# A fused two-layer transformer kernel: another order of work where the second attention meets the dense layers, and a last product in two halves

## The reference, cut to what matters

```python
x = x + _L0_xattn_ref(_layernorm(x), ctx_768, ...)
x = x + _L0_ffn_ref(_layernorm(x), ...)
x = x + _L1_xattn_ref(_layernorm(x), ctx_768, ...)   # 16 heads of 8 channels
x = x + _L1_ffn_ref(_layernorm(x), k0, k1, k2, s0, s1, s2)

def _L1_ffn_ref(x, k0, k1, k2, s0, s1, s2):
    # weights are +1 where k is true and -1 where it is false
    h = jnp.concatenate([x, -x], axis=-1)
    h = s0 * _conn_dense(k0, h)      # 256 -> 512
    h = jax.nn.relu(h) * 2
    h = s1 * _conn_dense(k1, h)      # 512 -> 512
    h = jax.nn.relu(h) * 2
    h = s2 * _conn_dense(k2, h)      # 512 -> 128
    return h
```

## Time and profile before

| what | value |
|---|---|
| median of three runs | 241.98 us |
| the profiled execution, its own time | 242.18 us |
| span of its instructions | 240.4 us |
| TensorE busy | 223.1 us (93%) |
| VectorE busy | 169.7 us (71%) |
| ScalarE busy | 123.0 us (51%) |
| mean granted TensorE clock | 0.998 |

### The profile page before, as it was taken

The page is one execution under the profiler, slowest core; times in us unless marked ns, Lnnn a source line. Parts: engine busy times, 40 slices in busy tenths (PEclk is TensorE's granted clock), DMA queues, the critical chain, the costliest instruction groups (busy, mean ns, idle before and its releaser), DMA issues.

```text
span 240.4 us, 4941 instructions
## 1 busy us (share of the span) xinstructions
PE 223.1 (93%) x1785; PEld 180.7 (75%) x1785; DVE 169.7 (71%) x438; ACT 123.0 (51%) x292; POOL 59.9 (25%) x87
## 2 busy tenths in 40 slices
PE   8988888989799999999999999999799999699993
PEld 8346677888787888898898899777578887477782
DVE  1699985768747796556555558988778887398752
ACT  2644669697864462212312324255356557547651
POOL 3272195006220124433033900260000000220200
PEclk9999999999999999999999999999999999999999
DMA  6940010000000002202102162000000000000002
GB/s 190 246 110 30 3 44 4 0 3 0 0 3 0 3 1 65 55 12 65 52 16 65 43 175 68 1 0 3 0 4 3 0 3 3 0 3 1 0 0 87
DMA packets 11820, 8.18 MB, mean 34 GB/s; under 512 B 2964, under 2 KB 11096, under 8 KB 11800
## 3 DMA queue, kind: packets, MB, share of 16 engines
q1 hardware_dynamic: 11800, 7.91, 12.6%
HBM read 5.81 MB, written 0.52 MB: 26 GB/s over the span
## 4 chain that ended last, share of the span: by engine, by line
PE 71%; DVE 13%; ACT 9%; issue 3%; DMA 2%; SPq 0%; DVEq 0%
PE ps L626 10%; PE ps L798 9%; PE ps L449 8%; PE ps L451 8%; PE ps L450 8%; ACT probs L907 6%; PE ps L540 3%; PE ps L717 3%; PE ps L745 3%; PE ps L445 3%; PE ps L704 3%; PE ps L520 3%; DMA x_sb<-in_x 2%; PE ps L730 2%; PE ps L758 2%
## 5 line engine op out<-in xcount | busy, mean ns | idle before, releaser
L956 ACT ACTIVATE kT<-ps 128x512 f32<-128x512 f32 x32 | 19.1, 598 | 47.4 <-PE ps L451 47.4
L626 PEld LDWEIGHTS ps<-w,kT 128*128 128x128 f32 x256 | 30.9, 192 | 1.2
L626 PE MATMUL ps<-w,kT 128*128 128x128 f32 x256 | 31.0, 275 | 0.0
L1273 DVE TENSOR_TENSOR kT<-ps,kT 128x512 f32<-128x512 f32 x32 | 21.8, 689 | 11.1 <-PE ps L451 8.8
L1280 DVE SCALAR_TENSOR_TENSOR x_sb<-ps,comb,x_sb 128x128 f32<-128x128 f32 x64 | 18.0, 343 | 13.5 <-PE ps L626 13.5
L449 PE MATMUL ps<-xT_hi,w_hi 128*128 128x512 f32 x64 | 26.7, 417 | 0.8 <-issue 0.6
L451 PE MATMUL ps<-xT_hi,w_lo 128*128 128x512 f32 x64 | 25.2, 393 | 0.0
L450 PE MATMUL ps<-xT_lo,w_hi 128*128 128x512 f32 x64 | 25.0, 390 | 0.0
L907 ACT ACTIVATE probs<-ps,negmax 128x128 f32<-128x128 f32 x64 | 22.7, 420 | 1.8 <-DVE negmax L1198 1.8
L1367 DVE TENSOR_REDUCE probs<-ps 128x8 f32<-128x1024 f32 x16 | 19.4, 1224 | 4.4 <-PE ps L704 4.3
L1002 ACT ACTIVATE probsT<-ps 128x1024 f32<-128x1024 f32 x16 | 16.5, 1029 | 9.7 <-PE ps L717 9.7
(11 more groups left out here) (190 smaller groups left out, 491.6 us busy)
## 6 DMA issues: line engine op xcount, KB each, us to landing
w_raw<-in_L_ffn_W SPq DMA_DIRECT2D x16, 128.0 KB, 2.2
k_st<-h_a SPq DMA_DIRECT2D x12, 128.0 KB, 2.7
w<-in_L_ffn_W SPq DMA_DIRECT2D x8, 128.0 KB, 2.1
x_sb<-in_x SPq DMA_DIRECT2D x1, 512.0 KB, 5.6
out<-qo SPq DMA_DIRECT2D x2, 256.0 KB, 2.4
ctx_sb<-in_ctx SPq DMA_DIRECT2D x1, 384.0 KB, 3.8
w_raw<-in_L_xattn_Wq SPq DMA_DIRECT2D x1, 256.0 KB, 5.8
wo<-in_L_xattn_Wo SPq DMA_DIRECT2D x1, 256.0 KB, 5.7
```

Source lines behind the costliest of these rows:

```text
L626: ins = pe.matmul(ps[:, 4 + slot, k * C:(k + 1) * C], uT[:, slot, c, k * P:(k + 1) * P], w3[:, buf, c, :], start=(c == 0), stop=(c == NH - 1))
L956: act.activation(silu[:, c, :], ps[:, c, :], ACT.Silu).then_inc(b_silu, 1)
L1273: dve.tensor_tensor(uT[:, slot, c, :], ps[:, 2 + c, :], silu[:, c, :], ALU.mult).then_inc(b_u, 1)
```

## The change

It has two parts.

**The join.** On TensorE unit 2 moves ahead of the turn of block 7's values, unit 3 ahead of block 7's second turn; the six constant matmuls ahead of unit 4 go, and four are put into unit 4 after its fourth matmul. On VectorE `ln_low(3, 0)` moves ahead of block 6's normalisation, `relu` of unit 1 ahead of block 7's normalisation and `relu` of unit 3 ahead of the last two residuals, with the low part of unit 1 between; the low part of unit 3 stays behind the residuals. For units 1 and 3 the two readers of the bank change places: VectorE's `relu` comes first and ScalarE's high part waits for it (`D_VECTOR_FIRST`). On ScalarE the high part of unit 2 moves ahead of block 7's `o1T`, its `relu` stays behind.

**The end.** The second half's last product (unit 17) becomes two of 256 columns in two banks, `d_last(1)` and `d_last(2)`; the turn of the first half's result, which stood behind the whole product, comes between them. Copy, turn, addition and store of the second half are two each as well, so there are three stores, of 256, 128 and 128 KB.

```diff
+        D_VECTOR_FIRST = (1, 3)
+        D_PARTS = ((0, slice(0, TG)), (1, slice(0, TG // 2)), (1, slice(TG // 2, TG)))
+        Y_BANK = (D_BANK[16 % ND], D_BANK[17 % ND], D_BANK[18 % ND])
+        Y_TURN = (6, 7, 0)
...
# SyncE
-            for t in range(NT):
-                sp.wait_ge(d_x, t + 1)
+            for n, (t, cols) in enumerate(D_PARTS):
+                sp.wait_ge(d_x, n + 1)
...
# TensorE, d_unit and c_step
+                    if n == 4 and i == 4:
+                        keep_busy(4, M0 + 1)
...
                 if s == NB:
                     d_unit(1)
+                    d_unit(2)
...
-                if s >= NB:
-                    d_unit(s - NB + 2)
+                if s == NB:
+                    d_unit(3)
...
-            keep_busy(6, M0 + 1)
-            for n in range(4, len(D_ORDER)):
+            for n in range(4, len(D_ORDER) - 1):
                 d_unit(n)
...
+            def d_last(part):
+                t, cols = D_PARTS[part]
+                for i in range(8):
+                    k, half = i // 2, i % 2
+                    if half == 0:
+                        pe.wait_ge(d_lo, lo_count(D_ORDER.index((1, t, k))))
+                    ins = pe.matmul(ps[:, Y_BANK[part], cols], d2_w[:, k, 0:P], h_at[1, t][:, half, k, cols],
+                                    start=(i == 0), stop=(i == 7))
+                ins.then_inc(d_ps, 1)
...
+            d_last(1)
+            d_turn(0)
+            d_last(2)
+            d_turn(1)
+            d_turn(2)
...
# ScalarE
+                if n in D_VECTOR_FIRST:
+                    act.wait_ge(d_relu_v, n // 2 + 1)
...
-            for s in range(NB + 2):
+            for s in range(NB + 1):
                 c_step(s)
+            d_high(2)
+            c_tail(NB - 1, 1)
+            d_whole(2)
...
# VectorE, c_step and d_whole
+                if s == NB - 1:
+                    ln_low(3, 0)
+                if s == NB:
+                    d_whole(1)
                 if 1 <= s <= NB:
                     c_normalise(s - 1)
...
-                if s == NB - 1:
-                    ln_low(3, 0)
+                if s == NB:
+                    d_low(1)
+                    d_whole(3)
                 if s == 2:
                     dve.wait_ge(xb1, NB)
                 if s >= 2:
                     c_residual(s - 2)
-                if s == NB:
-                    d_whole(1)
-                    d_low(1)
...
-                dve.wait_ge(d_hi, n + 1)
+                if n in D_VECTOR_FIRST:
+                    dve.wait_ge(d_ps, n + 1)
+                    dve.wait_ge(masks, 10)
+                else:
+                    dve.wait_ge(d_hi, n + 1)
```

More of the change, by code:

```diff
@@ L300, in _ @@
                     sp.dma_start(f32(k_st[p::NS, g, :]), f32(made[32 * g:32 * g + 32, :])).then_inc(k1_st, 16)
-            for t in range(NT):
-                sp.wait_ge(d_x, t + 1)
-                sp.dma_start(out[t * 4:t * 4 + 4].rearrange("b t c -> t b c"),
-                             fin[:, t, :].rearrange("p (b c) -> p b c", c=C)).then_inc(stored, 16)
-            sp.wait_ge(stored, 16 * NT)
+            for n, (t, cols) in enumerate(D_PARTS):
+                sp.wait_ge(d_x, n + 1)
+                b = 4 * t + cols.start // P
+                sp.dma_start(out[b:b + (cols.stop - cols.start) // P].rearrange("b t c -> t b c"),
+                             fin[:, t, cols].rearrange("p (b c) -> p b c", c=C)).then_inc(stored, 16)
+            sp.wait_ge(stored, 16 * len(D_PARTS))
         @block.gpsimd
@@ L858, in _, with d_turn @@
                 c_step(s)
-            keep_busy(6, M0 + 1)
-            for n in range(4, len(D_ORDER)):
+            for n in range(4, len(D_ORDER) - 1):
                 d_unit(n)
[L864 to L867, removed]
-                ins.then_inc(d_yT_ps, 1)
+            def d_last(part):
[7 more added lines that the diff above has]
+                ins.then_inc(d_ps, 1)
+            def d_turn(part):
+                t, cols = D_PARTS[part]
+                pe.wait_ge(d_yT, part + 1)
+                for c in range(cols.start, cols.stop, P):
+                    ins = pe.transpose(ps[:, Y_TURN[part], c:c + P], yT[:, t, c:c + P], ident[:, :])
+                ins.then_inc(d_yT_ps, 1)
+            pe.wait_ge(d_relu_v, (len(D_ORDER) - 1 - ND) // 2 + 1)
+            d_last(1)
[3 more added lines that the diff above has]
+            d_turn(2)
         @block.scalar
@@ L1029, in c_step, with d_high @@
                     c_query_signed(NG + 1)
-                if s >= NB - 1:
+                if NB - 1 <= s <= NB:
                     d_evacuate(s - NB + 1)
-            def d_evacuate(n):
+            def d_high(n):
                 layer, t, m = D_ORDER[n]
+                if n in D_VECTOR_FIRST:
+                    act.wait_ge(d_relu_v, n // 2 + 1)
                 act.wait_ge(d_ps, n + 1)
@@ L1040, in d_evacuate, with d_whole @@
                                scale=scale2[:, layer:layer + 1]).then_inc(d_hi, 1)
-                if n % 2 == 0:
[L1042 to L1046, removed]
+            def d_whole(n):
+                layer = D_ORDER[n][0]
+                if n >= ND + 4:
+                    m = n - ND
+                    act.wait_ge(d_lo_p if m in D_POOL else d_lo, lo_count(m))
+                act.activation(relu[:, n % ND, :], ps[:, D_BANK[n % ND], :], ACT.Relu,
+                               scale=scale2[:, layer:layer + 1]).then_inc(d_relu_a, 1)
+            def d_evacuate(n):
+                d_high(n)
+                if n % 2 == 0:
+                    d_whole(n)
             act.wait_ge(ln_nm, 1)
@@ L1060, in _ @@
                     ln_hi_copy(3, 1)
-            for t in range(NT):
-                act.wait_ge(d_ps, 16 + t + 1)
-                act.activation(yT[:, t, :], ps[:, D_BANK[(16 + t) % ND], :], ACT.Copy, scale=scale[:, 2:3]).then_inc(d_yT, 1)
+            for n, (t, cols) in enumerate(D_PARTS):
+                act.wait_ge(d_ps, 16 + n + 1)
+                act.activation(yT[:, t, cols], ps[:, Y_BANK[n], cols], ACT.Copy, scale=scale[:, 2:3]).then_inc(d_yT, 1)
         @block.vector
@@ L1455, in _ @@
                 c_step(s)
-            d_whole(3)
             d_low(3)
@@ L1467, in _ @@
                     d_low(n)
[L1468 to L1471, removed]
+            for n, (t, cols) in enumerate(D_PARTS):
+                dve.wait_ge(d_yT_ps, n + 1)
+                bs = slice(4 * t + cols.start // P, 4 * t + cols.stop // P)
+                dve.tensor_tensor(fin[:, t, cols], ps[:, Y_TURN[n], cols],
+                                  x_sb[:, bs, :].rearrange("p b c -> p (b c)"), ALU.add).then_inc(d_x, 1)
 _INS = ['x', 'ctx_768', 'L0_xattn_Wq', 'L0_xattn_Wk', 'L0_xattn_Wv', 'L0_xattn_Wo', 'L0_xattn_bo', 'L0_ffn_Wg',
```

## The result

Over 21 runs of each, the changed kernel takes 241.04 us in the median and the one before 242.57; the ratio is 0.9918 with a 95% interval of 0.9891 to 0.9945. That is 0.8% faster (0.5 to 1.1%), where 0.9% was forecast, and 241.04 lies near the upper end of the stated range of 238.8 to 241.2. The ratio is of fast runs alone: it leaves out, among others, runs of 276.19 and 1178.69 us of the changed kernel, without which its median is 240.38.

The account below looks back on a forecast made before the run. TensorE was taken to bound nearly everything from 203 us, with a 1.32 us wait and VectorE level with it before the transposes; 1.75 + 0.1 + 0.35 = 2.2 us gained gives 239.8 us, range 238.8 to 241.2.

Parts of the forecast that it names:

- The start of the join: With `ln_low` ahead of block 6's normalisation on VectorE, unit 0 starts at about 204.96 instead of 206.28: 1.3 us earlier.
- Block 7's tail and ScalarE's cover: Unit 2's 0.47 us on TensorE is hidden; `o1T` comes 1.36 us earlier, ScalarE being free 0.2 us before it is needed.
- VectorE to the root: VectorE's run from block 7's first residual to the second half's root takes 2.9 us; the root starts 2.45 us earlier.
- TensorE to the transposes: Unit 4 starts at 210.53, the transposes at 216.2 with TensorE, not `xn`, the limit; the join gives 1.75 us.
- The end: From unit 17's start to the last addition's end: 4.12 us by sum instead of 4.18, called 0.1 us gained.
- The last store: Behind the last addition 128 KB remain instead of 256; 0.35 us gained, ends none and about 0.45.
- ScalarE late: Rival, 0.18 less favoured at 0.12: ScalarE's wait for VectorE's `relu` delays `o1T`; the join gives 1.1 us, time 240.4.
- the end that pays for itself: Rival, chance 0.18: the turn between the halves, a second wait and the third store eat the halving; 240.2 to 240.6 us.
- VectorE's limit: Rival, chance 0.14: unit 4 starts sooner, so VectorE's 2.45 us is the limit at the join; time 239.1 us.
- The clock: Rival, chance 0.06: TensorE falls to half clock in units 4 to 6, costing 5.6 us; time 245.4 us.

Follow-up runs that it names:

- e6: The changed kernel with `ln_low` of the first half back behind block 6's normalisation on VectorE; 34.94 us from block 6's turn to the end, against 33.56.
- e7: The changed kernel with ScalarE's high part again before VectorE's `relu` for units 1 and 3; 36.69 us from block 6's turn to the end, against 33.56.
- e9: The changed kernel with GpSimd's low part of unit 2 waiting for VectorE's of unit 3; 34.56 us from block 6's turn to the end, against 33.56.
- e5: The changed kernel without the four constant matmuls inside unit 4; ratio 0.9874, 32.97 us from block 6's turn to the end, against 33.56.
- e4: The changed kernel with the turn of the first half's result behind both halves of the last product; ratio 0.9938, slower than the changed kernel by 0.64 us.
- e8: The changed kernel with one 256 KB store for the second half, behind both additions; 2.72 us from the last addition to the end, against 2.27.
- e11: The changed kernel without the constants, units 4 and 5 alternating by four matmuls; ratio 0.9858, 32.87 us from block 6's turn to the end, against 33.56.
- e12: e11 with the second half's joined statistics in front of unit 3's low part on VectorE; ratio 0.988, 32.59 us from block 6's turn to the end.

## Why the prediction was right

The steps came in the forecast order and nearly at the forecast sizes. In the trace all three parts of the sum came out a little larger: 1.84, 0.14 and 0.54, in sum 2.53 us up to the end, for 1.75 + 0.1 + 0.35 = 2.2. That the ratio of the whole runs, 0.8% or 2.0 us, lies so near the forecast's 0.9% is in part luck, since its interval runs from 0.5 to 1.1%. It is also less than the 1% that the prediction itself calls what such a measurement can tell from no change; the anchored traces, not the whole runs, show where the time went.

*The start of the join.* Right: unit 0 1.44 us sooner where 1.3 was forecast (unit 0 starts 0.13 before the end that the turn's row gives), and e6 loses 1.38 without this move.

*Block 7's tail and ScalarE's cover.* Right, with less to spare than thought: 0.2 us forecast, nearly nothing measured, and no delay. The prediction did not price the exchange of the readers. By e7, set back to full clock by the estimate above, the new positions without it gain nothing up to the transposes; with the fall of the clock that came in e7 they are worse than the old ones, 36.69 against 36.09. What the other moves are worth one by one (units 2 and 3 on TensorE, each `relu` on VectorE) was not tested.

*VectorE to the root.* The term was mis-sized: 2.45 us forecast, 2.19 measured. The step took each operation at the duration it had in the old surroundings. Moved, unit 3's low part falls on GpSimd's of unit 2 and takes 0.35 longer (1.04 for 0.69; 0.68 in e9). It cost the time nothing, since TensorE was the limit there.

*TensorE to the transposes.* Right: unit 4 at 6.09 (6.22 forecast), the transposes at 11.80 (11.9), with `xn` ready before. The join gave 1.84 where the sum has 1.75. The low parts were in time, as worked out, but only behind the constants: without them (e5) TensorE waits for both, so that of the 0.93 us that the constants take no more than 0.55 to 0.59 is won back.

*The end.* 0.14 us against 0.1. Addition: 0.42 as interpolated; copy: 0.47, above the 0.42. The turn between the halves, which the sum booked as a cost of 0.55, is what lets the first store go early; without it the last addition ends only 0.07 sooner (e4).

*The last store.* Mis-sized: 0.54 us, 0.35 forecast. e8 puts 0.45 on the size, the upper end of the estimate. That end took the store of 256 KB to have a fixed part of some 1.5 us, which no row gives. The formula of the Trainium skill that the prediction sets beside it (DMA: Bandwidth & Descriptors, Anatomy of one DMA) is stated there for transfers that GpSimd issues; these are issued by SyncE, and its 0.3 is short of the 0.45.

*The rivals.* ScalarE late and the end that pays for itself did not come. VectorE's limit did not come either: unit 4 started only 0.13 us sooner than forecast, and TensorE reached the transposes 0.52 behind `xn`. The clock did not fall there in the trace of the changed kernel, but it did in e7, in this place: the price there was 1.27 us and not 5.6, as the clock came back inside unit 4 and did not stay down for 24 matmuls.

## What to carry to other kernels

Look in the chain for waits without work, and then in the timeline for an operation whose input was complete long before it started: undoing the move of one such operation ahead of one that has to wait anyway cost 1.4 us here. When two engines run level, work out both after a move, and price each moved operation with what will run beside it. Look at the granted clock behind every new idle stretch of TensorE. A store cut in two pays when the part behind the last operation gets smaller while the other parts leave early.

## What the runs showed of the hardware

VectorE's subtraction with both inputs in SBUF took 0.69 us alone and 1.04 when it began while GpSimd's subtraction was running (the changed kernel, e5, e6 and e11: 1.03 to 1.04); residuals and `relu`, which read PSUM, did not slow (0.27 and 0.75 beside GpSimd's in the changed kernel). In e12, where only its first 0.21 us ran beside GpSimd's, it took 0.75. The Trainium skill (SBUF — State Buffer, Who interferes with whom) says that a VectorE instruction with two SBUF inputs contends with a GpSimd instruction that reads SBUF; these traces agree, with 0.37 us at the root in e9. The count of inputs is not all, though: in e9 a `TENSOR_SCALAR` with a single tensor input, in SBUF, took 1.15 us instead of 0.17 and ended 0.04 after GpSimd's.

TensorE idle for 1.32 us kept its clock; idle for 1.65 us in e7, from 210.99 to 212.64, it was granted half from about 212.1 to 215.5, and the eight matmuls of 512 columns from unit 4's start (four of the unit, four constants) took 215.90 - 212.64 = 3.26 us, where at full clock 8 x 0.2335 = 1.87 are due. These are two single gaps in one execution each, not a bound.
